# Two graph layers on one Trainium2 core: whole-tile residues and a ring of four split tiles in the third sweep

## What is computed

```
def layer0(x, adj, W, b):
    d = sum(adj, axis=1)
    s = 1 / (sqrt(d) + 1e-8)
    return (adj * s[:, None] * s[None, :]) @ (x @ W + b)

def layer1(x, adj, W, b):
    a = adj + eye(8192)
    s = 1 / sqrt(sum(a, axis=1))
    return relu((a * s[:, None] * s[None, :]) @ (x @ W) + b)

x = layernorm(x + layer0(x, adj, W0, b0))
x = layernorm(x + layer1(x, adj, W1, b1))
```

## Time and profile before

| what | value |
|---|---|
| median of 3 runs | 1884.22 us (1883.65 to 1885.18) |
| the profiled execution's own time | 1884.51 us |
| its span | 1882.3 us |
| TensorE busy over the span | 1655.4 us (88%) |
| VectorE busy | 1264.2 us (67%) |
| ScalarE busy | 739.5 us (39%) |
| mean granted TensorE clock | 0.964 of full speed |
| sweep 3 | from about 1439 us to 1867 us |

### The profile page before, as it was taken

One profiled execution on the slowest core, in us unless ns is written; L12 is line 12 of the kernel. 1 busy time (PEld: TensorE's weight loads), 2 busy tenths in 40 slices (PEclk: granted clock), 3 DMA queues, 4 the chain that ended last, 5 costly groups with the idle time before them and its releaser, 6 DMA issues.

```text
span 1882.3 us, 17109 instructions
## 1 busy us (share of the span) xinstructions
PE 1655.4 (88%) x6136; PEld 1117.6 (59%) x6136; DVE 1264.2 (67%) x1854; ACT 739.5 (39%) x889; POOL 66.2 (4%) x127
## 2 busy tenths in 40 slices
PE   0257889999999999968999999999999999999996
PEld 0123344444444444456777777787787787777775
DVE  1444556776876567277655656545547899999996
ACT  5553342111000000045444444444446666666663
POOL 0000000000000000000000000000000000000000
PEclk9778899999999999989999999999999999999998
DMA  9999999998877976155666665656567999999991
GB/s 387 421 421 421 421 422 393 416 404 343 366 312 290 367 298 232 28 213 212 250 232 227 229 227 209 213 219 228 196 216 313 421 397 363 353 356 361 362 367 78
DMA packets 85906, 573.38 MB, mean 305 GB/s; under 512 B 10400, under 2 KB 10656, under 8 KB 20288
## 3 DMA queue, kind: packets, MB, share of 16 engines
q1 hardware_dynamic: 76320, 541.23, 72.6%
q0 software_dynamic: 9504, 31.07, 4.7%
HBM read 556.79 MB, written 15.47 MB: 304 GB/s over the span
## 4 chain that ended last, share of the span: by engine, by line
PE 67%; DVE 18%; DMA 11%; issue 3%; ACT 1%; SPq 0%; DVEq 0%; POOL 0%; ACTq 0%
PE acc L659 28%; PE acc L683 12%; PE acc L685 12%; PE acc L684 12%; DVE low L806 7%; DMA lent<-adj_tiles 6%; DMA own<-adj_tiles 2%; DVE stats L781 1%; DMA own<-adj_far 1%; DMA lent<-adj_far 1%; DVE run L817 1%; DVE o L795 1%; PE turned L595 1%; DVE z L930 1%; DVE h L884 1%
## 5 line engine op out<-in xcount | busy, mean ns | idle before, releaser
L683 PE MATMUL acc<-high,feat_high 128*128 128x512 f32 x1336 | 536.1, 401 | 70.6 <-DVE low L806 59.5
L659 PE MATMUL acc<-lent,feat 128*128 128x512 f32 x1168 | 522.8, 607 | 20.9 <-DVE feat L856 13.5
L685 PE MATMUL acc<-high,feat_low 128*128 128x512 f32 x1336 | 526.7, 394 | 0.0
L684 PE MATMUL acc<-low,feat_high 128*128 128x512 f32 x1336 | 525.9, 394 | 0.0
L806 DVE TENSOR_TENSOR low<-own,high 128x1024 fp32r<-128x1024 f32 x330 | 390.5, 1220 | 177.7 <-ACT high L702 175.1
L702 ACT CAST high<-own 128x1024 fp32r<-128x1024 f32 x330 | 338.2, 1052 | 197.1 <-PE acc L685 190.4
L659 PEld LDWEIGHTS acc<-lent,feat 128*128 128x128 f32 x1168 | 226.2, 195 | 304.5 <-issue 288.6
L817 DVE TENSOR_TENSOR run<-run,lent 128x2048 f32<-128x2048 f32 x135 | 309.3, 2291 | 135.8 <-DMA lent<-adj_tiles 129.7
L683 PEld LDWEIGHTS acc<-high,feat_high 128*128 128x128 f32 x1336 | 254.1, 190 | 139.2 <-issue 81.5
L685 PEld LDWEIGHTS acc<-high,feat_low 128*128 128x128 f32 x1336 | 254.0, 190 | 55.2
L684 PEld LDWEIGHTS acc<-low,feat_high 128*128 128x128 f32 x1336 | 254.5, 191 | 50.1
(11 more groups left out here) (77 smaller groups left out, 649.3 us busy)
## 6 DMA issues: line engine op xcount, KB each, us to landing
lent<-adj_tiles SPq DMA_DIRECT2D x237, 1024.0 KB, 11.1
own<-adj_tiles SPq DMA_DIRECT2D x197, 1024.0 KB, 5.6
lent<-adj_far SPq DMA_DIRECT2D x60, 1024.0 KB, 23.0
own<-adj_far SPq DMA_DIRECT2D x18, 1024.0 KB, 23.0
x_in<-x_rows POOLq DMA_DIRECT2D x32, 256.0 KB, 4.4
sums_rows<-stage POOLq DMA_DIRECT2D x27, 256.0 KB, 6.4
sums_in<-sums_rows POOLq DMA_DIRECT2D x27, 256.0 KB, 6.3
x_t<-x_cols SPq DMA_DIRECT2D x16, 256.0 KB, 15.6
```

The costliest lines, as they stand in the source:

```text
L659: mm = nc.tensor.matmul(bank, feat0[:, j * Q + q, :], raw(n)[:, q * T:(q + 1) * T], start=(u == plan.first[g] and q == 0), stop=(u == plan ...
L683: nc.tensor.matmul(bank, f_high, a_high[:, chunk], start=(u == plan.first[g] and q == 0), stop=False)
L684: nc.tensor.matmul(bank, f_high, a_low[:, chunk], start=False, stop=False)
L685: mm = nc.tensor.matmul(bank, f_low, a_high[:, chunk], start=False, stop=(u == plan.last[g] and q == Q - 1))
```

## The change

In sweep 3 VectorE does one subtraction of 128 x 2048 for a tile, in place of two of 128 x 1024. It waits for both halves of `high`, and adds 2 to `low_ready` when it is done. The memory is shared out anew: `LENT3_SLOTS` goes from 6 to 4, which frees 16 KB a partition, and `MORE` from 2 to 4, which takes them; the ring then holds four whole tiles. ScalarE still writes `high` by halves, and TensorE still waits and releases by halves. The ring's last buffers follow each other in pairs, which the new assertion states. Sweeps 1 and 2 keep their instructions.

```diff
--- before.py
+++ after.py
@@ -15,9 +15,9 @@
 FAR_PARTS = 4
 OWN_SLOTS = 3
 LENT1_SLOTS = 16
-LENT3_SLOTS = 6
+LENT3_SLOTS = 4
 RING = 4
-MORE = 2
+MORE = 4
 AHEAD = {1: 0, 2: 0, 3: 1}
 BANKS = 6
 SCALE_LAG = 1
@@ -223,6 +223,12 @@
                 self.buffer.append(b)
                 self.half_before.append(where.get(b, first_use[b[0] == 3]))
                 where[b] = 2 * u + half
+
+
+        for u in range(self.end):
+            if self.loads[self.takes[u][0]][0] == 3:
+                (ring0, b0), (ring1, b1) = self.buffer[2 * u], self.buffer[2 * u + 1]
+                assert ring0 == ring1 and b1 == b0 + 1
 
 
         self.landings, seen = [], [0] * len(holds)
@@ -798,7 +804,15 @@
 
             in_row = 0
             for kind, i in plan.dve:
-                if kind == "low":
+                if kind == "low" and loads[takes[i][0]][0] == 3:
+                    n = takes[i][0]
+                    ring, b = plan.buffer[2 * i]
+                    dve.wait_ge(high_ready, 2 * (i - plan.natives) + 2)
+                    nc.vector.tensor_tensor(low_ring[ring][:, b:b + 2, :].rearrange("p b n -> p (b n)"), raw(n),
+                                            high_ring[ring][:, b:b + 2, :].rearrange("p b n -> p (b n)").bitcast(F32),
+                                            ALU.subtract).then_inc(low_ready, 2)
+
+                elif kind == "low":
                     n = takes[i][0]
                     for half in range(2):
                         m = 2 * i + half
```

## The result

The changed kernel takes 1892.93 us (median of 5 runs, 1892.79 to 1892.96), the kernel before 1884.41 beside it. The ratio is 1.0045, 95% interval 1.003 to 1.0059: slower by 8.5 us, where 7.4 were forecast. The profiled execution has a span of 1890.8 us, also 8.5 more.

A forecast was written before the change was run, and what follows sets the result against it. The prediction took sweep 3 to be bound by VectorE's row work, the first `low` after it, then TensorE alone. Nine cycle terms, +0.53 to +1.14 us, summed to +7.4 us, giving a median of 1891.6 us, range 1883 to 1898.

The forecast's parts named there:

- The bound: Sweep 3: a chain of `y_t`, VectorE's row work, the first `low` after it, then TensorE alone to the next `y_t`.
- The price of 1.07 us a cycle, less 0.067 for each `low` on the way: Sweep 3: TensorE starts 1.07 us later each cycle; each whole `low` since the cycle's first `y_t` returns 0.067 us.
- the deciding `low`: Sweep 3: the first `low` after VectorE's row work, whose end releases TensorE's last wait in a cycle; 1.07 us later.
- `low` now waits for both halves of `high` costs nothing: VectorE's row work in sweep 3: ScalarE had made both halves earlier, so the wait adds 0.
- Row 5, sized too low: Sweep 3, row 9 to 8: only row 6's `y_t` was foreseen late, by 0.2 us; that cycle +1.14 us.
- The ring, counted at 0: Sweep 3: a fourth whole tile adds nothing to TensorE's stock when row work begins; 0, at the bounds 1 us back.
- The slots, counted at 0: Sweep 3 loads: seven raw slots instead of nine still let tiles land in time; 0, bound 0 to +4 us.
- The clock, counted at 0 with a bound of 4 x 1.4 us: TensorE in sweep 3: longer waits may lower its clock, 1.4 us each where nothing hides it; bound 0 to +5.6 us.
- TensorE's wait: Sweep 3: TensorE's total wait for `low` was to rise from 24.7 to about 35 us.
- the wait before the tile ahead of the deciding one: TensorE in row 14's cycle, sweep 3: the wait of 2.55 us was to grow to about 2.8 us.
- VectorE is the bound (rival a): Sweep 3: VectorE sets the time, so the saving counts in full, 9.1 us less, 1875; chance 0.10.
- both cancel (b): Sweep 3: saving and delay cancel, or the fourth tile covers the later `low` in most cycles: 1881 to 1888; chance 0.11.

The follow-up runs named there:

- The two fillers: Changed kernel plus two unused VectorE additions at each of seven rows: before `y_t` of rows 14 to 8, 1896.12 us; behind `make_out` of rows 0 to 6, 1913.44 us.
- the run with the filler in the row work: Changed kernel plus two unused 128x512 VectorE additions right behind `make_out` of rows 0 to 6: 1913.44 us, ratio 1.0146 to the kernel before.

## Why the prediction was right

**The bound.** That VectorE, 95% busy, is not what sets the sweep was read from who waits last. The two fillers show it: 1.5 us of VectorE cost nothing (0.05 us each) in one place and 1.5 us or more in the other.

**The price of 1.07 us a cycle, less 0.067 for each `low` on the way.** The measured distance from the start of the deciding `low` to TensorE is 2.44 us against 1.36 before. Five cycles (rows 0 to 14, and 14 to 10) were forecast at 3.68 in sum and came to 4.15. Most of what is missing is a small term that I didn't have: behind `y_t` the whole `low` starts 0.22 us after the end of `y_t` (1540.69 + 0.69 to 1541.60), a half 0.14 us (1538.91 + 0.69 to 1539.74):

```profile
1539.74 2.36 DVE L806 TENSOR_TENSOR low<-own,high 128x1024 fp32r<-128x1024 f32 x2
```

At one or two such places a cycle (none in row 0's) that is 0.07 or 0.14; with it 14 to 13 becomes 0.87, 13 to 12 0.88, 12 to 11 0.81 and 11 to 10 0.74, against 0.87, 0.87, 0.76 and 0.75 measured. The prediction's "1024 columns at 1.067 ns" is a slip: 1.067 us for all 1024 columns gives the 2.29 that it states and the trace shows, and nothing else hangs on it.

**The step that failed in part: "`low` now waits for both halves of `high` costs nothing".** It held in the row work, but not at the start of the sweep, where 1.07 became 1.49. ScalarE there has two copies of TensorE's small products in its list, `x_t` (L753) and `feat_high` (L757), and `high` of u3 and u4 stands behind them. VectorE and TensorE there:

```profile
1438.49 6.69 DVE L811 TENSOR_TENSOR low<-lent,high 128x2048 fp32r<-128x2048 f32 x3
1446.99 2.29 DVE L811 TENSOR_TENSOR low<-lent,high 128x2048 fp32r<-128x2048 f32 x1 [1.81 <-ACT high L708]
...
1451.20 6.70 DVE L811 TENSOR_TENSOR low<-own,high 128x2048 fp32r<-128x2048 f32 x3 [0.83 <-ACT high L708]
```

```profile
1453.63 0.47 PE L689 MATMUL acc<-high,feat_high 128*128 128x512 f32 x1 [0.15 <-DVE low L811]
```

TensorE ends u0 later, so its transposes, ScalarE's copies and `high` of u4 come later, that `low` waits for the second half of `high` as well (0.83 us), and TensorE waits for it at 1453.63 although u0's `low` should have been the last to decide. That matmul starts 0.53 us behind the one before it, where 0.23 is the pace: 0.30 of the 0.42 us.

**Row 5, sized too low.** I foresaw that row 6's `y_t` would come to wait for TensorE (0.72 us measured). Row 5's did too, 0.22 us, which I had left out. The two cycles were forecast at 1.67, would be 1.95 with the gap behind `y_t`, and gave 2.48. Counted from row 10's `y_t`, row 5's comes at 20.04 us (1748.18 to 1768.22). VectorE's own pace would have it at 19.75: 20.08 in the kernel before, less 6 x 0.067, plus 0.07 for the gap. That is 0.29 us. Row 6's, counted from row 9's, comes 0.40 us later than before, where I had 0.2. The two make up nearly all of it.

**The ring, counted at 0.** Right with halves. With whole tiles the fourth tile gives 1.6 us in the sweep, since with three the `low` behind `y_t` waits for `high`. As the change brings both, the sum didn't suffer.

**The slots, counted at 0.** Right: seven slots gave no more than longer waits of ScalarE, all before row 15's `y_t`, and none in mid-sweep.

**The clock, counted at 0 with a bound of 4 x 1.4 us.** In the profiled execution of the changed kernel the clock fell only where the next wait hid it, as before: behind the wait of 2.52 us that ended at 1507.79 (0.84 in the window 1505 to 1510). The next tile's `low`, started at 1509.81, let TensorE go on no earlier than 1512.24 anyway. Its loss where nothing hides it is shown by other runs, 1.6 to 2.8 us a cycle, more than the 1.4 that I bounded it by.

**Luck in the number.** The terms add up to 7.4 us and the sweep lost 9.1. The start of the sweep (0.4), the gap behind `y_t` (0.5) and rows 5 and 6 (0.8) were missing, all on the same side. The 8.5 us of the spans lie nearer the forecast only because this execution reached the sweep 0.6 us earlier. TensorE's wait came to 32.3 us, not 35: the wait before the tile ahead of the deciding one was expected to grow to 2.8 us and stayed at 2.52.

**VectorE is the bound (rival a), both cancel (b).** Both fell, with the medians outside them. Of the two sides of the rule that the prediction weighed from the Trainium skill (Perfetto Trace Analysis, section Optimizing Scalar/DVE Operations), grouping for a saturated engine and breaking up for one that causes bubbles, the second is the one that this sweep followed. That section ties it to an engine that isn't saturated; here VectorE was 94 to 95% busy in the windows of the earlier trace rows, and the waits decided.

## What to carry to other kernels

Merging two instructions saves their fixed cost on the producer and delays the consumer by the length of the second one; which counts is read from the wait that ends last in each cycle, not from the share of busy time. If the consumer has work that doesn't need the late operand, put that first: here the same instructions in another order were worth 18 us on the changed kernel and 9.5 on the one before, while the merge lost 8.5. When a wait is taken off one tile, work out the next tile as well, since the whole one behind it becomes the late one.

## What the hardware showed that I had not expected

TensorE at 1802.09 in the run with the filler in the row work, and that run's window 1445 to 1450:

```profile
1802.09 0.47 PE L689 MATMUL acc<-high,feat_high 128*128 128x512 f32 x1 [2.96 <-DVE low L815]
```

```profile
1445.00:1450.00 5.00, 5.00 (x17) 4.02 (x15) 2.41 (x2) 0.50 (x2) 0.91 (x2) 0.57 1.02 414
```

The same window of the changed kernel:

```profile
1445.00:1450.00 5.00, 5.00 (x28) 4.25 (x27) 3.19 (x5) 3.82 (x7) 1.65 (x3) 1.00 1.02 429
```

The granted clock of TensorE did not follow the length of one wait alone. In the run with the filler in the row work, the first matmul behind a wait of 2.97 us, at 1573.02, was slow at once (0.77 us instead of 0.47); behind one of 2.96 us at 1802.09 it was not, and that cycle was longer by the filler alone. After 2.6 us it fell in some executions and not in others at the same place of the program: in the first tiles of the sweep the window behind such a wait showed 0.57 and 0.75 in the two filler runs and 1.00 in the changed kernel. What decides between them these runs don't show.

A subtraction behind `y_t` started 0.07 us later when it was 2048 columns wide than with 1024. The width alone doesn't do it: in the kernel before, an instruction of 4 columns behind row 1's `y_t` also started 0.22 us after its end. What takes the time stays open.

```profile
1548.55 0.17 DVE L774 TENSOR_SCALAR sdev<-sdev 128x4 f32<-128x4 f32 x1 [0.22 <-DVE y_t L915]
```
